# A two-layer graph network on one core: first-layer halves transposed by DMA with a lag of two tiles, and two diffusion tiles moved from the second step to the first

## What is computed

```python
h = relu(layernorm(x))                       # then layer 0: a quantised graph convolution
x1 = x + (adj @ quantised(relu(quantised(h) @ quantised(W))))

X = relu(layernorm(x1))                      # layer 1: two steps of diffusion
R = (adj + I) / rowsum(adj + I)
Xf, Xa, Z = X, X, 0
for s in range(2):
    A = top_p_softmax(Xa W1 W2 W3' Xa')      # 2048 x 2048, only the top 0.9 of the mass is kept
    Xf, Xa = R @ Xf, A @ Xa
    Z += Xf @ U1[s] + Xa @ U2[s]
out = x1 + layernorm(X + Z) * gamma + beta   # as the last layer's residual
```

## Time and profile before

| | us |
|---|---|
| median of 3 runs | 1202.13 (1200.91 to 1208.22) |
| the profiled execution | 1202.94 |
| its span, first to last instruction | 1201.2 |
| layer 0, tiles 2 to 14, by line 1532 | 116 to 284, 14.0 each |
| step 0, from the first logits | from 312 |
| step 1: DVE's work from the exponentials on | from 785 |

### The profile page before, as it was taken

How to read it: one execution, slowest core, us unless ns; L and a number is a source line. 1 busy time by engine, 2 the same in 40 slices (tenths; PEclk the granted TensorE clock), 3 DMA queues, 4 the chain that set the end, 5 groups by cost and what they waited for, 6 DMA issues and landing times.

```text
span 1201.2 us, 16645 instructions
## 1 busy us (share of the span) xinstructions
PE 1097.6 (91%) x5402; PEld 513.7 (43%) x5402; DVE 989.4 (82%) x2144; ACT 483.9 (40%) x920; POOL 286.8 (24%) x255
## 2 busy tenths in 40 slices
PE   0478999999899969999999998989899999999987
PEld 0234454455434434444444444434344444444433
DVE  7877777776389999889999800889999999999997
ACT  1764444443743213453532223874003364351061
POOL 6124333333132311211121210131111111112143
PEclk9898999999999989999999998999899999999999
DMA  7054565553243453163164084023667467576667
GB/s 263 26 192 163 182 211 192 201 200 144 73 141 109 147 131 80 45 149 71 45 151 93 22 175 140 36 80 122 223 208 166 92 186 140 176 195 151 236 143 217
DMA packets 190708, 171.68 MB, mean 143 GB/s; under 512 B 144736, under 2 KB 144736, under 8 KB 186528
## 3 DMA queue, kind: packets, MB, share of 16 engines
q1 hardware_dynamic: 190624, 170.71, 49.5%
HBM read 87.84 MB, written 49.28 MB: 114 GB/s over the span
## 4 chain that ended last, share of the span: by engine, by line
DVE 32%; PE 30%; issue 18%; POOL 7%; ACT 6%; DMA 5%; SPq 1%; POOLq 1%; DVEq 0%; ACTq 0%
PE AB L987 5%; PE RB L987 5%; DVE WS L1605 4%; DVE cand L1837 4%; PE UB L816 4%; DVE WS L1834 3%; PE XB L816 3%; PE AB L989 3%; DVE E L1850 3%; PE RB L989 2%; DMA turns<-E 2%; DVE rows L1685 2%; DVE WS L1842 2%; DVE E L1572 2%; DMA AD<-xu_d 2%
## 5 line engine op out<-in xcount | busy, mean ns | idle before, releaser
L1685 DVE TENSOR_REDUCE rows<-E 128x1 f32<-128x2048 f32 x32 | 73.0, 2281 | 86.0 <-ACT E L1221 85.8
L682 POOL TENSOR_TENSOR RT<-RT,AD 128x512 f32<-128x512 f32 x32 | 55.7, 1739 | 256.9 <-ACT RT L1281 256.8
L1605 DVE SCALAR_TENSOR_TENSOR WS<-E,rows 128x2048 bf16<-128x2048 f32 x43 | 110.6, 2613 | 0.4
L1837 DVE MAX8 cand<-WS 128x8 f32<-128x128 f32 x512 | 102.1, 278 | 1.1
L1842 DVE SCALAR_TENSOR_TENSOR WS<-E,rows 128x2048 f32<-128x2048 f32 x32 | 79.4, 2482 | 0.8
L696 POOL TENSOR_TENSOR XX<-WF,XX 128x512 f16<-128x512 f32 x16 | 26.4, 1651 | 222.8 <-ACT XX L1306 222.8
L1850 DVE SCALAR_TENSOR_TENSOR E<-WS,E 128x2048 f16<-128x2048 f32 x32 | 77.1, 2410 | 2.2 <-issue 1.1
L1834 DVE SCALAR_TENSOR_TENSOR WS<-E,rows 128x2048 f32<-128x2048 f32 x32 | 77.3, 2415 | 1.1
L987 PE MATMUL RB<-XR,turns 128*128 128x512 f16 x256 | 62.1, 387 | 11.3 <-DMA turns<-E 11.3
L1258 ACT ACTIVATE E<-E,nmx 128x2048 f32<-128x2048 f32 x32 | 63.7, 1992 | 5.7 <-DVE nmx L1686 5.7
L987 PE MATMUL AB<-VR,turns 128*128 128x512 f16 x256 | 61.4, 383 | 4.6 <-DMA turns<-E 4.6
(11 more groups left out here) (343 smaller groups left out, 2194.5 us busy)
## 6 DMA issues: line engine op xcount, KB each, us to landing
turns<-adj_parts SPq DMA_DIRECT2D x48, 512.0 KB, 4.0
E<-adjT SPq DMA_DIRECT2D x16, 1024.0 KB, 7.6
adj_parts<-turns SPq DMA_DIRECT2D x16, 1024.0 KB, 5.2
AH<-adj_parts SPq DMA_DIRECT2D x16, 512.0 KB, 4.3
z_d<-UO SPq DMA_DIRECT2D x28, 256.0 KB, 2.3
XR<-x SPq DMA_DIRECT2D x4, 1024.0 KB, 11.8
WS<-U SPq DMA_DIRECT2D x4, 1024.0 KB, 5.3
x_d<-WF SPq DMA_DIRECT2D x16, 256.0 KB, 2.1
```

The lines of the kernel that those rows point to most:

```text
L1605: return v.scalar_tensor_tensor(junk[t % 2], e, g4[:, k, t:t + 1], e, op, ALU.mult, accum_out=g4[:, F_, t:t + 1])
L1685: ct(v.tensor_reduce(row(A2)[:, t:t + 1], E[:, slot, :], AX.X, ALU.max))
L1837: i = v.max(cand[:, t, 8 * c:8 * c + 8], WS[:, c * PART:(c + 1) * PART])
```

## The change

Three things.

First, XF's halves of layer 0 are transposed by DMA. `x0_turn(t)` on SP waits for `x_lo(t)` (and until the buffer of two tiles ago is free) and issues one DMA transpose of 128 x 1024 16-bit numbers from `XR` into one of two buffers, `XT` and a free piece of `E`. PE's 8 matmuls and ACT's copy are gone. Its place on SP is between `l0_stores(t)` and `at_out(t + 1)`.

Second, `post0` runs two tiles behind layer 0, not one.

Third, `R_LATE` is 2 and `R_BEHIND` is ((1, 2, 1, 1), (1, 3, 3, 2)): step 0 has one more diffusion tile ahead of group 0 and one more ahead of group 1; step 1 has one fewer ahead of group 2 and one fewer ahead of group 3. At the start of step 1 there are still nine, two of rs = 0 and seven of rs = 1. The reload of `XR` from DRAM at the start of step 1 is made in two pieces.

The core of the diff (the removed PE and ACT functions are cut to their calls):

```diff
-R_LATE = 4
-R_BEHIND = ((0, 1, 1, 1), (1, 3, 4, 3))
+R_LATE = 2
+R_BEHIND = ((1, 2, 1, 1), (1, 3, 3, 2))
@@ SP
+            def x0_turn(t):
+                sp.wait_ge(s_xh, t + 1)
+                sp.wait_ge(s_xl, t + 1 + OPEN)
+                if t < 2:
+                    sp.wait_ge(s_mm1, T + OPEN)
+                else:
+                    sp.wait_ge(s_pk, t - 1)
+                sp.dma_start_transpose(x0_turned[t % 2].rearrange("p h k c -> p (h k) c"),
+                                       XR[:, t, :, :].rearrange("p h d -> p (h d)")).then_inc(s_x0T[t % 2], 16)
             def l0_tile(t, odd):
                 l0_stores(t)
+                x0_turn(t)
                 at_out(t + 1, odd)
-                adj_in(t + 3)
+                if t + 3 < T:
+                    adj_in(t + 3)
                 diag_out(t)
-                post0_stores(t - 1)
+                if t >= 2:
+                    post0_stores(t - 2)
 ...
             l0_stores(0)
+            x0_turn(0)
             at_out(1, 1)
             adj_in(3)
             diag_out(0)
             u_in(3)
 ...
             l0_stores(T - 1)
+            x0_turn(T - 1)
+            post0_stores(T - 3)
             post0_stores(T - 2)
@@ SP, start of step 1
-                sp.dma_start(XR[:, 0:T - R_LATE, ...], v_parts[0:T - R_LATE]...)
+                v_rows(slice(0, POSTPONED))
 ...
+                sp.wait_ge(s_u, 2 * T)
+                v_rows(slice(POSTPONED, T - R_LATE))
@@ PE
-                    if j == T // 4 and n is not None:
-                        x_halves_turned(n)
 ...
-            def post0(n):
-                pe.wait_ge(s_xTc, n + 1)
+            def post0(n, odd, last=False):
+                halves = halves_of_turned(x0_turned[odd])
+                pe.wait_ge(s_x0T[odd], 8 * n - 8 * odd + 16)
 ...
-            with pe.Fori(1, T - 1, 2) as odd:
-                layer0(odd, 1)
-                layer0(odd + 1, 0)
-            layer0(T - 1, 1)
-            x_halves_turned(T - 1)
-            post0_last(T - 1)
+            with pe.Fori(2, T, 2) as even:
+                layer0(even, 0)
+                post0(even - 2, 0)
+                layer0(even + 1, 1)
+                post0(even - 1, 1)
+            post0(T - 2, 0)
+            post0(T - 1, 1, True)
@@ ACT
-            def l0_tile(t):
+            def l0_head(t):
                 turn_free(t + 1)
                 adj_hi(t + 1)
-                xT_halves(t - 1)
-                post0(t - 1)
 ...
-            l0_tile(1)
+            l0_head(1)
+            x_hi(1)
+            l0_head(2)
+            post0(0, 2)
             u_hi(3)
-            with act.Fori(2, T - 1) as t:
-                l0_tile(t)
-            xT_halves(T - 2)
+            with act.Fori(3, T - 1) as t:
+                l0_head(t)
+                post0(t - 2, t)
```

More of the change, by code:

```diff
@@ L243, in build @@
         s_part = sem("s_part")
+        s_x0T = [sem(f"s_x0T{odd}") for odd in range(2)]
         s_sqd = sem("s_sqd")
@@ L390, in _ @@
             u_in(3)
-            for t in range(1, T - 3):
+            for t in range(1, T - 1):
                 l0_tile(t, (t + 1) % 2)
[L393 to L397, removed]
             sp.wait_ge(s_mm2, T - 1)
@@ L670, in _ @@
             u_lo(2)
-            l0_tile(1)
+            l0_head(1)
+            l0_tile(2)
             u_lo(3)
-            with pool.Fori(2, T) as t:
+            with pool.Fori(3, T) as t:
                 l0_tile(t)
+            v_lo(T - 2, of(VR, T - 2))
+            pk_lo(T - 2, 0, T - 2, s_vl, T - 1)
             pk_lo(T - 1, 0, T - 1, s_vl, T - 1)
@@ L855, in x_rest, with halves_of_turned, pk_product @@
                 less(XB, x_turned_of(n)[:, 0, :, :].rearrange("p k c -> p (k c)"), minus).then_inc(s_xTs, 1)
+            def halves_of_turned(u):
+                return [lambda k, h=h: u[:, h, k, :] for h in range(2)]
             def halves_turned(n):
-                return [lambda k, h=h: x_turned_of(n)[:, h, k, :] for h in range(2)]
-            def pk_product(n, bank):
-                hi, lo = halves_turned(n)
+                return halves_of_turned(x_turned_of(n))
+            def pk_product(n, bank, halves=None):
+                hi, lo = halves or halves_turned(n)
                 three(bank[:, 0:P], lambda k: WPK[:, k, 0, :], lambda k: WPK[:, k, 1, :], hi, lo).then_inc(s_pk, 1)
-            def post0(n):
-                pe.wait_ge(s_xTc, n + 1)
+            def post0(n, odd, last=False):
+                halves = halves_of_turned(x0_turned[odd])
+                pe.wait_ge(s_x0T[odd], 8 * n - 8 * odd + 16)
+                if last:
+                    pe.wait_ge(s_pkc, n + OPEN)
+                    pk_product(n, XB, halves)
                 pe.wait_ge(s_ue, n + OPEN)
-                three(UB[:, :], xh, xl, lambda k: U10p[:, k, 0, :], lambda k: U10p[:, k, 1, :]).then_inc(s_u, 1)
+                three(UB[:, :], *halves, lambda k: U10p[:, k, 0, :], lambda k: U10p[:, k, 1, :]).then_inc(s_u, 1)
                 pe.wait_ge(s_ve, n + OPEN)
[L872 to L882, removed]
+                three(RB[:, :], *halves, lambda k: U11p[:, k, 0, :], lambda k: U11p[:, k, 1, :]).then_inc(s_v, 1)
+                if not last:
+                    pe.wait_ge(s_wpk, 4)
+                    pe.wait_ge(s_pkc, n + OPEN)
+                    pk_product(n, XB, halves)
             pe.wait_ge(s_sup, NG)
@@ L1178, in v_hi, with post0 @@
                 a(VR[:, bass.ds(t, 1), 0, :].rearrange("p o d -> p (o d)"), RT[:, :], ACT.Copy).then_inc(s_vh, 1)
-            def post0(t, last=False):
+            def post0(t, x=None, last=False):
                 if last:
@@ L1185, in post0 @@
                 a(UO[:, :], UB[:, :], ACT.Copy, scale=SV / (SX * SW)).then_inc(s_ue, 1)
-                if not last:
-                    x_hi(t + 1)
+                if x is not None:
+                    x_hi(x)
                 act.wait_ge(s_v, t + 1)
@@ L1207, in _ @@
             x_hi(0)
-            l0_tile(1)
+            l0_head(1)
+            x_hi(1)
+            l0_head(2)
+            post0(0, 2)
             u_hi(3)
-            with act.Fori(2, T - 1) as t:
-                l0_tile(t)
-            xT_halves(T - 2)
+            with act.Fori(3, T - 1) as t:
+                l0_head(t)
+                post0(t - 2, t)
+            post0(T - 3, T - 1)
             post0(T - 2)
-            xT_halves(T - 1)
-            post0(T - 1, True)
+            post0(T - 1, last=True)
             def logits_out(qq, slot, chunks=range(NC)):
```

51 lines of the change are left out of this document (21 added, 30 removed).

## The result

The changed kernel takes 1282.2 us (median of 4, 1281.38 to 1284.79) where the kernel before, beside it, takes 1204.86 (a fourth execution added to the three that gave 1202.13). The ratio is 1.0647, with a 95% interval of 1.0604 to 1.069: slower, as forecast, but by 77 us and not by 53, and 4 us outside the range (1231 to 1278). The span of the profiled execution went from 1201.2 to 1279.9, by 78.7.

What follows compares the result with a forecast made beforehand. The prediction took a ring through the diagonal block's store to bound layer 0, PE step 0 and DVE step 1. 1202.94 + 44.8 (layer 0) + 8.1 (step 0) + 0 (step 1) = 1255.9, forecast 1255, range 1231 to 1278.

Steps and rivals of the forecast that it cites:

- The ring: Layer 0, DVE's line 1532 through x1, `at_out`, slab load and `diag_out` to the next line 1532: 17.79 us for 13.97, 11 turns, 42.0 us.
- the wait for the block's store: Layer 0, each tile: DVE waits some 4 us at line 1532 for the store of the diagonal block.
- the two opposite corrections: Layer 0's ring: earlier store of x1 makes it 17.0 us, the transpose's landing added makes it 19.7; neither taken.
- The tail of layer 0: End of layer 0: one more `post0` against a wait for the last transposes that goes away, between 0 and 3, 1 us taken.
- Step 0: Extra diffusion tile fills PE's hole ahead of group 0 (-1.1 us), the one ahead of group 1 costs 9.2: 8.1 us more.
- Step 1: Nine diffusion tiles stand at its start; PE's 20.7 us less ahead of groups 2 and 3 only lengthens its wait: nothing.
- rival 1: Layer 0 is not slowed, since the block's store lands in time anyway: 1205, no change; chance 0.07.
- rival 2: Layer 0: the block's landing shrinks by 1 to 2.5 us, ring 15.3 to 16.8: 1223 to 1240; chance 0.11.
- Rival 3: PE, not DVE, sets step 1, so the two tiles that leave bring up to 20.7 us: 1235; chance 0.12.
- Rival 4: Layer 0: PE's clock falls after its waits; at 1.2 GHz for a whole tile 86 us more, 1341; chance 0.03.
- PE's hole ahead of the high-half product: Sign in a tile of layer 0: PE stands some 4 to 5 us there, with a granted clock below 1.
- PE's wait at the last group: Sign in step 1: PE waits near 24 us at the last group, not 3.8.

## Why the prediction was wrong, point by point

**Sign and mechanism.** Right. The ring was named with its members and its place, the wait for the block's store was forecast at some 4 us and is 4.5 to 5.2, and the two runs that cut it, one by SP's order and one by buffers, gave the tile back at 14.1 and 13.8 us.

**The size of the ring: mis-sized by 0.5 us a turn.** The sum had 17.79; one turn of the trace is 18.12, and the mean of the eleven is 18.38, or 18.28 without the longest. `x_lo` was right (7.91, measured 7.92). The transpose and its gaps took 1.44 us for 1.35, and from `at_out` to the next block line it is 8.76 for 8.53: the sum of the two opposite corrections, the store of x1 leaving earlier and the transpose still in flight, is small, as assumed; no run shows the two apart. One turn, from tile 2 to 3, took 19.4 us. The kernel before has such a turn too, of 19.3 us, but from tile 1 to 2, ahead of the stretch that was counted: ACT makes the last weight's halves in it (`u_hi(3)`) ahead of `adj_hi`, and DVE waits for the slab's half. In the changed kernel that work comes one tile later, and the forecast had no term for it. In all 48.2 us for 42.0.

**The tail of layer 0: mis-sized.** 4.3 us more for the 1 that was taken, and outside the 0 to 3 given. 0.4 of it is the turn from tile 13 to 14 (14.1 us for 13.7), which was put at nothing. For the rest the step at fault is the one more `post0` that was set "against a wait for the last transposes that goes away". Three `post0` now follow the last product, and they go through one UO buffer. ACT waits 4.2 us for the store of the UO before, and PE 3.7 us for ACT, as the trace has it; no run takes this wait away:

```profile
357.38 0.60 ACT L1192 ACTIVATE UO<-UB 128x512 f32<-128x512 f32 x1 [4.24 <-DMA xu_d<-UO]
```

```profile
360.48 0.83 PE L839 MATMUL XB<-E,WPK 128*128 128x128 f16 x12 [3.67 <-ACT Khl L1182]
```

**Step 0.** Right: 8.2 us for 8.1, PE's hole ahead of group 0 gone, the second tile ahead of group 1 at close to its full price.

**Step 1: the step that failed.** "At its start nine diffusion tiles stand as before" counted PE's work and not its order against ACT. With two late tiles instead of four, the tile that the second round needs comes two tiles, some 21 us, earlier in PE's program, while the exponentials ahead of its copy on ACT come at the same time as before. On SP the forecast named what is queued behind a waiting instruction; on ACT it did not. The step was put at nothing and cost 17.1 us. Of the 26 us between the forecast and the profiled execution (1255.9, 1281.96), 17.1 are this step's, 6.2 the ring's and 3.3 the tail's. Step 1's loss alone would have given 1272, inside the range; it took layer 0's 9.5 us as well to leave it.

**The rivals.** That layer 0 is not slowed (rival 1): out; the block's store lands 7.5 us after its issue, where it landed 7.3, so the landing did not shrink. With it rival 2 is out (its own ring gives some 1226 to 1242, not 1223 to 1240; nothing hangs on that). Rival 3, that step 1 gains from two tiles less: out; run with ACT's order mended, step 1 is as long as before, where PE's two tiles less would have made it 20.7 us shorter. Rival 4, the clock: in the tile shown, behind a hole of 5.4 us, the granted clock is 0.50 (1.2 GHz) from 249.47 to 252.00 and 1.00 (2.4 GHz) from 254.6 on. PE's first 16 matmuls take 5.30 us and the next 16 take 3.62, and the loss stays inside the wait, as the forecast had it; the clock comes back within the tile.

**What was to be seen.** The ring, the granted clock below 1 and step 0 came as told. PE's hole ahead of the high-half product was forecast at 4 to 5 us and is 2.1 to 5.4, 3.5 in the mean; in the tile shown the slower first 16 matmuls take another 1.7 us. PE's wait at the last group, forecast near 24 us, is 11.4, with 8.5 more ahead of group 2's second tile and 23.4 at the start of the step: the work that left did turn into waiting, but at three places, and the first of them was on the path. The 8.5 us are SP's order once more: DVE had kept that tile by 1142.0, and SP issued its transposes at 1158.7, behind the store of a diffusion tile. It costs nothing while DVE sets the step's pace.

## What to carry to other kernels

Before an instruction is put into an in-order queue, write down the time at which its wait ends and look at every later entry whose completion somebody needs within one period. Here 1.3 us of issue and 2.5 us of wait made each tile 4 us longer, and moving one line or adding two small buffers takes it back. The same holds for compute engines when work is taken out of a schedule: a copy that stood safely behind a waiting operation becomes late when its producer comes earlier, so the place of such an operation is to be counted in time, not in tiles. And removing work from an engine that is busy 99% of the time is worth nothing as long as another ring is as long as its period.

## What the runs showed of the hardware that was not expected

A DMA transpose in the queue ahead of plain transfers slowed them little here: from the issue of the slab's store to DVE's next block line it was 8.53 us without and 8.76 us with the transpose issued 1.4 us before it. The store of x1 left earlier at the same time, by the prediction's estimate worth 0.8 us, so the transpose's own share may be up to 1 us.

What stands ahead of a small store sets when it lands. The block's store landed 7.3 us after its issue (median) behind the slab's store and load, and 2.0 us after it when it was issued ahead of them.

The issue of a transpose took SP 1.26 us (median) in the changed kernel, 1.7 to 1.8 us right behind a slab's store and load (the run with the block first and the transposes), and 2.4 to 2.5 us with the block's store between them as well (the run with the transpose last).

DVE and POOL slowed each other in the run with the slab's half early: 0.28 to 1.25 us for DVE's 128 x 128 add, and 1.16 to 3.16 us for POOL's subtraction of 128 x 512, when they ran side by side. In the run before it the same subtraction lay beside DVE's reduction (line 1522, 216.21 to 219.96) and took 1.16 us. The cause was not tested apart.
